# Reciprocals and their remainder in PSUM, exponentials earlier in ScalarE's order, softmax sums one token tile earlier

## The reference

```python
qh = (q @ Wq + bq).reshape(Bn, Tq, H, DK)
kh = (k @ Wk + bk).reshape(Bn, Tk, H, DK)
vh = (v @ Wv + bv).reshape(Bn, Tk, H, DK)
attn = jnp.einsum('bqhd,bkhd->hbqk', qh, kh) * mask[None]
attn = attn - jnp.max(attn)
attn = jnp.exp(attn) * mask[None]
attn = attn / (jnp.sum(attn, axis=-1, keepdims=True) + 1e-15)
out = jnp.einsum('hbqk,bkhd->bqhd', attn, vh).reshape(Bn, Tq, H * DK)
x = out @ Wo + bo + residual
# layer norm of x over its 512 columns, times gamma, plus beta
```

## Time and profile before

| What | us |
|---|---|
| median of 3 runs | 1820.88 (1820.13 to 1823.03) |
| the profiled execution | 1822.08, its span 1820.3 |
| output phase in it | 923 to 1820 |
| one unit, from `residual` 3 to the next `residual` 3 | 27.19 to 27.20 |

### The profile page before, as it was taken

One profiled execution on the slowest core, in us unless ns is written; L12 is line 12 of the kernel. 1 busy time (PEld: TensorE's weight loads), 2 busy tenths in 40 slices (PEclk: granted clock), 3 DMA queues, 4 the chain that ended last, 5 costly groups with the idle time before them and its releaser, 6 DMA issues.

```text
span 1820.3 us, 30538 instructions
## 1 busy us (share of the span) xinstructions
PE 1692.9 (93%) x11008; PEld 850.1 (47%) x11008; DVE 1321.0 (73%) x2218; ACT 780.5 (43%) x1029; POOL 700.7 (38%) x647
## 2 busy tenths in 40 slices
PE   4989999999999999999959999999999999999997
PEld 4545455564555555555414444444444444444443
DVE  7746565456555556464548899899899899989986
ACT  6744555555555545455433233233233233333330
POOL 0000000000000000000016878788788788788788
PEclk8999999999999999999969999999999999999999
DMA  7372552644534453542353554644554544554521
GB/s 220 139 266 91 194 190 85 239 147 164 173 138 173 156 217 112 190 171 102 139 181 139 231 207 163 230 170 157 226 207 167 225 178 153 223 207 173 219 93 70
DMA packets 81469, 315.01 MB, mean 173 GB/s; under 512 B 5392, under 2 KB 9616, under 8 KB 71696
## 3 DMA queue, kind: packets, MB, share of 16 engines
q1 hardware_dynamic: 81424, 314.41, 47.0%
HBM read 184.37 MB, written 130.02 MB: 173 GB/s over the span
## 4 chain that ended last, share of the span: by engine, by line
DVE 30%; issue 11%; PE 3%; ACT 3%; POOL 2%; DVEq 1%; POOLq 0%; ACTq 0%
DVE s L909 6%; DVE p_lo L914 6%; DVE stats L926 5%; DVE y L923 4%; DVE r L892 3%; DVE y L933 2%; ACT p_hi L848 2%; DVE rest L896 1%; PE ps_o L71 1%; PE ps_o L70 1%; PE ps_o L72 1%; POOL rstd L1011 1%; DVE r_all L903 1%; DVE mean_var L928 1%; ACT r_hi L840 1%
## 5 line engine op out<-in xcount | busy, mean ns | idle before, releaser
L70 PE MATMUL ps_s<-x_hi,g_hi 128*128 128x512 f16 x1024 | 388.4, 379 | 6.0 <-ACT s L485 6.0
L70 PE MATMUL ps_o<-u,p_hi 128*128 128x512 f16 x1024 | 389.8, 381 | 0.0
L71 PE MATMUL ps_o<-u,p_hi 128*128 128x512 f16 x1024 | 389.4, 380 | 0.0
L72 PE MATMUL ps_o<-u,p_lo 128*128 128x512 f16 x1024 | 389.3, 380 | 0.0
L71 PE MATMUL ps_s<-x_lo,g_hi 128*128 128x512 f16 x1024 | 388.1, 379 | 0.0
L72 PE MATMUL ps_s<-x_hi,g_lo 128*128 128x512 f16 x1024 | 388.1, 379 | 0.0
L991 POOL PARTITION_ALL_REDUCE key_max<-score_max x1 | 0.4, 377 | 923.1 <-issue 923.1
L848 ACT ACTIVATE p_hi<-s 128x1024 f16<-128x1024 f32 x128 | 135.3, 1057 | 439.2 <-DVE s L909 439.2
L485 ACT ACTIVATE s<-ps_s,c_bias 128x512 f32<-128x512 f32 x256 | 175.9, 688 | 333.2 <-PE ps_s L72 329.3
L594 DVE TENSOR_TENSOR score_max<-score_max,tile_max 128x1 f32<-128x1 f32 x257 | 40.7, 158 | 338.1 <-ACT s L485 335.8
L914 DVE TENSOR_TENSOR p_lo<-s,p_hi 128x1024 f16<-128x1024 f32 x128 | 224.3, 1752 | 15.8 <-ACT p_hi L848 15.8
(11 more groups left out here) (82 smaller groups left out, 2493.2 us busy)
## 6 DMA issues: line engine op xcount, KB each, us to landing
scores<-s SPq DMA_DIRECT2D x30, 2048.0 KB, 7.6
s<-scores SPq DMA_DIRECT2D x30, 2048.0 KB, 8.0
x<-xT_in SPq DMA_DIRECT2D x32, 1024.0 KB, 9.7
u_halves<-u_out SPq DMA_DIRECT2D x64, 512.0 KB, 2.9
u<-u_halves SPq DMA_DIRECT2D x16, 2048.0 KB, 11.7
y<-x_in SPq DMA_DIRECT2D x32, 1024.0 KB, 10.3
out<-y SPq DMA_DIRECT2D x31, 1024.0 KB, 4.2
mask<-maskT_in SPq DMA_DIRECT2D x32, 256.0 KB, 10.3
```

Source lines behind the costliest of these rows:

```text
L70: pe.matmul(out, lhs_hi, rhs_hi, start=first, stop=False)
L71: pe.matmul(out, lhs_hi, rhs_lo, start=False, stop=False)
L72: return pe.matmul(out, lhs_lo, rhs_hi, start=False, stop=last)
```

## The change

Three things change in the output phase. `r32` and `rest`, which were SBUF tensors, become two halves of the PSUM bank `ps_sum`: `rest` takes columns 0 to 255, where the sums were before they were read, and `r32` columns 256 to 511. Since `rest` now lies where the next sums go, `sums` waits for `r_all_done` instead of `den_done`, and the counts of that semaphore shift by one. ACT's order becomes round 0, exps 0, round 1, exps 1, round 2, round 3, round_r, where it was round 0, 1, 2, exps 0, round 3, exps 1, round_r. And `sums` moves from place (3, 2) to (2, 2), ahead of spreads 6 and 7. The number of instructions stays the same.

```diff
--- before.py
+++ after.py
@@ -665,13 +665,15 @@
         y32 = sb("y32", [P, UNITS, TB, D])
         gamma_b, beta_b, bo_b = sb("gamma_b", [P, D]), sb("beta_b", [P, D]), sb("bo_b", [P, D])
         part = sb("part", [P, 2])
-        den, r32, rest = sb("den", [P, HT]), sb("r32", [P, HT]), sb("rest", [P, HT])
+        den = sb("den", [P, HT])
         r_hi, r_mid, r_all = sb("r_hi", [P, HT], BF16), sb("r_mid", [P, HT], BF16), sb("r_all", [P, HT], BF16)
         stats, mean_var = sb("stats", [P, TB, 6]), sb("mean_var", [P, TB, 2])
         var_eps, rstd, minus_half = sb("var_eps", [P, TB]), sb("rstd", [P, TB]), sb("minus_half", [P, 1])
         ln_eps = sb("ln_eps", [P, 1])
 
+
         ps_sum = bank("ps_sum")
+        r32, rest = ps_sum[:, HT:2 * HT], ps_sum[:, 0:HT]
         ps_bc = [bank(f"ps_bc{i}") for i in range(2)]
         ps_o = [bank(f"ps_o{i}") for i in range(OBANKS)]
 
@@ -693,7 +695,7 @@
 
 
         spread_at = {(0, 2): 0, (0, 5): 1, (1, 0): 2, (1, 3): 3, (1, 6): 4, (2, 1): 5, (2, 4): 6, (2, 7): 7}
-        sums_at = (3, 2)
+        sums_at = (2, 2)
 
         def tokens(a, b, u):
 
@@ -769,7 +771,7 @@
             def sums(n, s):
 
 
-                pe.wait_ge(den_done, n + 1)
+                pe.wait_ge(r_all_done, n + 1)
                 for i in range(4):
                     if i % 2 == 0:
                         pe.wait_ge(exp_done, 2 * n + i // 2 + 1)
@@ -783,7 +785,7 @@
             def spread(n, p):
 
                 if p == 0:
-                    pe.wait_ge(r_all_done, n + 1)
+                    pe.wait_ge(r_all_done, n + 2)
                 pe.wait_ge(p_scaled, n * NP + p + 1)
                 for th in range(2):
                     mm = pe.matmul(ps_bc[p % 2][:, th * HT:(th + 1) * HT], sel_bc[:, p, th, :], r_all[:, :],
@@ -837,9 +839,9 @@
 
             def round_r(n):
                 act.wait_ge(r_done, n + 1)
-                act.activation(r_hi[:, :], r32[:, :], ACT.Copy).then_inc(r_hi_done, 1)
+                act.activation(r_hi[:, :], r32, ACT.Copy).then_inc(r_hi_done, 1)
                 act.wait_ge(rest_done, n + 1)
-                act.activation(r_mid[:, :], rest[:, :], ACT.Copy).then_inc(r_mid_done, 1)
+                act.activation(r_mid[:, :], rest, ACT.Copy).then_inc(r_mid_done, 1)
 
             def round_p(n, s, k):
                 if k == 0:
@@ -854,14 +856,16 @@
                     more, more2 = not (last and u == UNITS - 1), not (last and u >= UNITS - 2)
                     if more:
                         round_p(n + 1, s, 0)
-                        round_p(n + 1, s, 1)
-                        round_p(n + 1, s, 2)
                     if more2:
                         exps(n + 2, u, 0)
                     if more:
+                        round_p(n + 1, s, 1)
+                    if more2:
+                        exps(n + 2, u, 1)
+                    if more:
+                        round_p(n + 1, s, 2)
                         round_p(n + 1, s, 3)
                     if more2:
-                        exps(n + 2, u, 1)
                         round_r(n + 2)
 
             act.wait_ge(max_done, 1)
@@ -879,7 +883,7 @@
 
         @block.vector
         def _(dve):
-            dve.sem_inc(den_done, 1)
+            dve.sem_inc(r_all_done, 1)
             dve.sem_inc(p_scaled, 2)
             dve.sem_inc(p_lo_done, 8)
             dve.sem_inc(y_added, OBANKS)
@@ -888,19 +892,19 @@
 
                 dve.wait_ge(e_summed, n + 1)
                 dve.tensor_scalar(den[:, :], ps_sum[:, 0:HT], TINY, None, ALU.add).then_inc(den_done, 1)
-                dve.wait_ge(den_done, n + 2)
-                dve.reciprocal(r32[:, :], den[:, :]).then_inc(r_done, 1)
+                dve.wait_ge(den_done, n + 1)
+                dve.reciprocal(r32, den[:, :]).then_inc(r_done, 1)
 
             def second_part(n):
                 dve.wait_ge(r_hi_done, n + 1)
-                dve.scalar_tensor_tensor(rest[:, :], r_hi[:, :], part[:, 0:1], r32[:, :], ALU.mult, ALU.add)\
+                dve.scalar_tensor_tensor(rest, r_hi[:, :], part[:, 0:1], r32, ALU.mult, ALU.add)\
                    .then_inc(rest_done, 1)
 
             def third_part(n):
                 dve.wait_ge(r_mid_done, n + 1)
                 if not (isinstance(n, int) and n == 0):
                     dve.wait_ge(r_spread, n * NP)
-                dve.scalar_tensor_tensor(r_all[:, :], r_mid[:, :], part[:, 1:2], rest[:, :], ALU.mult, ALU.add)\
+                dve.scalar_tensor_tensor(r_all[:, :], r_mid[:, :], part[:, 1:2], rest, ALU.mult, ALU.add)\
                    .then_inc(r_all_done, 1)
 
             def scale_p(n, s, p):
```

## The result

| | before | after |
|---|---|---|
| median of 17 runs, us | 1820.51 (1818.93 to 1823.88) | 1825.45 (1822.18 to 1829.65) |
| profiled execution, its span, us | 1822.08, 1820.3 | 1825.01, 1823.2 |
| busy time of DVE, us | 1321.0 | 1277.2 |
| mean granted clock of TensorE | 0.985 | 0.975 |

The ratio is 1.0027, with a 95% interval of 1.0019 to 1.0034: slower by 0.27%, where 0.45% faster was forecast (8.2 us of 1820.88). DVE is busy 44 us less, and the kernel is 5 us slower.

A forecast was written before the change was run, and what follows sets the result against it. DVE, without slack, was taken to set the period: 0.13 us later at `split_p` 3's end, 0.43 less behind it, 0.30 shorter per unit. Over 29 units 8.7 us, net 8.2 with the first unit, gave 1812.7; range 1786 to 1830.

The forecast's parts named there:

- 1.: PSUM operands on DVE: L896 falls from 0.93 us to 0.41 to 0.48, next start after 0.37 us, 0.49 us less.
- 2.: ACT's order: exps 0 and 1 come earlier and delay no rounding, with some 0.9 us to spare.
- 3.: Sums at (2, 2) on PE: 1.79 us wait gone, sums cost 2.08 us ahead of spread 7, `scale_p` 7 waits 1.10 us.
- step 4: DVE from `residual` 2 to `split_p` 3: split takes 1.22 us, not 2.29, and ends only 0.13 us later despite the wait.
- step 5: DVE behind `split_p` 3: `norm` 2 loses to POOL's L1003; `residual` 3 starts 4.83 us after the split's end, now 5.26.
- 6.: First unit of the loop, where DVE already waits for PE: `scale_p` 6 and 7 move 2.0 us, unit 0.5 us longer.
- C: Slower: new wait at `scale_p` 7 is not absorbed; unit 0.70 us longer, 20 us in 29, 1842; chance 0.15.
- Rival A: `norm` 2 on DVE goes in front of POOL's L1003; unit 1.19 us shorter, 1787 for the median; chance 0.22.

The follow-up runs named there:

- the better order: PSUM operands, ACT's new order, sums at (3, 2), `residual` 3 moved up, against the kernel before: 1823.93 us; with spreads 0 and 1 later too: 1747.94 us.

## Why the prediction was wrong

The forecast was 1812.7, the result 1825.45. The step that failed is the one that put PE's idle time at nothing ("a wait of PE is worth something only if somebody waits for PE") and so made 29 equal units out of one. In 10 of the 29 the granted clock fell behind that idle time, the spreads came late, and DVE did wait for PE: 1.38 us at scale 2 and 1.47 us at scale 7 in the slow unit from 1443.06 on:

```profile
1449.70 0.69 DVE L913 TENSOR_TENSOR s<-s,ps_bc 128x512 f32<-128x512 f32 x1 [1.38 <-PE ps_bc L791]
...
1462.47 0.69 DVE L913 TENSOR_TENSOR s<-s,ps_bc 128x512 f32<-128x512 f32 x1 [1.47 <-PE ps_bc L791]
```

I had the cause in my hands: "PE idle about 2.1 us before spread 0, where its freed time goes" stands there as a sign that the forecast is right, and was booked at nothing. Measured, it is 2.05 us, and in 10 of 29 units it costs 1.24 us. The run with four fill matmuls shows this directly: with nothing else changed than PE's idle time, the slow units vanish and 12.3 us with them.

The kernel before had a warning of it in its trace. The granted clock of 1.00 given for 949.6 to 1767 us is a rounded mean, and it hides the first unit of the loop. PE had stood idle for 3.65 us before spread 0 there, and in the windows view the first 4 us behind it look like this:

```profile
950.00:954.00 4.00, 3.78 (x10) 1.49 (x11) 0.77 (x2) 0.00 (x0) 0.00 (x0) 0.50 0.95 381
```

That idle time is longer than the 2.05 us here, so it was a hint and no more.

By the steps:

1. L896 takes 0.49 us instead of 0.93, with 0.40 us to the next start where I took 0.37. Right. ACT's two roundings went from 417 to 383 ns, within the bound of 0.05 us.
2. ACT's order: no rounding is late, and all 32 sum matmuls run in one go, 1.93 us (the earlier trace rows show two halves with 1.79 us between). Right.
3. Sums at (2, 2): from spread 5 to spread 6 it takes 4.13 us (1482.38 to 1486.51) instead of 2.16, so the sums cost 1.97 us, forecast 2.08. The wait at scale 7 is 0.91 us, forecast 1.10. Right in kind, 0.1 and 0.2 us too large.
4. `norm` 1 takes 0.76 us (forecast 0.67), split 3 takes 1.21 us instead of 2.29, and it ends 22.07 us behind `residual` 3 (1493.23 less 1471.16), which is the forecast value (1463.24 less 1441.17). The absorption of the new wait is shown.
5. `norm` 2 is held (1.50 us) and the next `residual` 3 starts 4.79 us behind the end of split 3, forecast 4.83. The outcome was right; the reason, a needed lead in recorded starts, fell with the two runs with a memset.
6. The first unit of the loop: 28.82 us between its two `r_all`, against 28.97 before. I had it 0.5 us longer. It was 0.15 us shorter, 0.7 us in all.

One wait was missing from my account of DVE, which "idles only in short round trips". The longest in the unit is this one, at `norm` 3, for POOL's 1/std:

```profile
1443.77 1.48 DVE L933 TENSOR_SCALAR y<-y,mean_var,rstd 128x512 f32<-128x512 f32 x1 [0.94 <-POOL rstd L1011]
```

It is 0.93 us in the changed kernel, so it does not touch the sum, but it is what the better order took away.

So the clean unit was forecast at 26.9 us and took 26.86, though step 5 was right by a rule that does not hold. The sum over the units came out with the wrong sign all the same, since a third of them were not clean. Of the rivals, C named PE as the new bound and had the right sign, but by another mechanism: it wants the wait at scale 7 not absorbed, and it was (step 4). DVE's waits for `ps_bc`, 60.9 us in all and 7.7 before, look as C describes and are no proof of it. Rival A's place, `norm` 2 ahead of POOL, is what PSUM alone reached: 25.95 us a unit. The prediction asked only whether a few hundredths could win it. It did not ask what the parts would do one by one: with split 3 still held by POOL, `add_bo` comes at e + 3.21 and `norm` 2, at e + 2.98, goes first; with the moved sums split 3 is short, `add_bo` comes at e + 2.94, and `norm` 2 is held. The two go together in the five kernels with PSUM operands, `residual` 3 where the change leaves it, and no memset: `norm` 2 is held in the changed kernel and in those with the fill and with spread 0 later, and free in the two with the sums unmoved. What decides between them is open.

The Trainium skill, TensorE: Matmul & The Clock Gate, section HAM oscillation — how this bites in real kernels, describes a kernel whose matmuls wait for data and come back at the lower clock, again and again. The traces agree in kind, with waits of 1.95 to 2.4 us in a kernel whose PE is busy 93% of its span. The prediction had weighed PE's waits only by who waits for PE.

## What to carry to other kernels

A wait on an engine that is not the bound is free only if it stays short: on TensorE, several waits of 0.2 to 1.8 us joined into one of 2 us or more can cost more than they ever did apart. So when an edit frees time on TensorE, write down where the idle time will lie and how long it will be in one piece, and move work (here the first spreads) into it. Parts of a change are not additive, where each decides in which gap of a third engine the others' instructions fall: PSUM operands gave 36 us alone and nothing clear of noise beside the moved sums, so try the parts alone before the whole. And an order of service between two engines that is read from recorded starts is a guess until a run moves one of them.

## What the runs showed of the hardware

How often the granted clock fell behind PE's idle time before spread 0, in the 29 units behind the first of the loop:

| Kernel | idle time, us | fell |
|---|---|---|
| changed | 2.05 to 2.08 | 10 of 17 |
| changed | 1.73 to 1.86 | 0 of 12 |
| ACT's order alone | 2.31 to 2.40 | 11 of 17 |
| ACT's order alone | 1.37 to 1.46 | 0 of 12 |
| all but the PSUM operands | 1.93 to 2.27 | 7 of 29 |
| `residual` 3 moved up | 1.85 to 1.97 | 12 of 29 |

The shortest idle time with a fall behind it was 1.95 us. There was no fall behind the 1.79 us in the sums of the kernel before, nor in the runs with fill matmuls (1.1 to 1.2 us in nearly all units). So the length of the idle time does not settle it alone: of 90 idle times of 1.93 us and more 40 had a fall behind them, and in none of the four traces did two slow units follow each other. What else decides is open. In the slow units the nine matmuls and the spread behind the wait took 3.4 to 3.9 us instead of 2.17. The 17 runs of the changed kernel spread over 7.5 us and the four with the fill over 1.6 us; but ten runs of ACT's order with five fills, which had no slow unit in its trace, spread over 6.6 us, so the spread doesn't tell the two kinds apart.

ACT reads 256 float32 columns from PSUM in 383 ns and from SBUF in 417. The reciprocal of 256 columns takes 1.76 us into PSUM and 1.75 into SBUF. The remainder takes 0.49 us with one operand in PSUM, as in SBUF where POOL is silent (0.48), so what PSUM saves DVE there is the hold by POOL and nothing else.
